# Softmax attention in one long stream: second-pass scores one position earlier, preparation spread over forty positions, first-pass scores multiplied twice

## The reference, cut to what matters

```python
sim = einsum('bhid,bhjd->bhij', q, k) / sqrt(hd)      # 4 sequences, 16 heads of width 8, n = 1024
sim = where(causal, neg, sim)
p = softmax(sim);  entropy = -sum(p * log(p + 1e-9))
beta = where(entropy > 0.5, maximum(poly(entropy), 1.0), 1.0)
attn = softmax(sim * beta)                            # a second softmax over the same scores
out = (attn @ v) @ Wo.T + bo
```

## Time and profile before

| what | us |
|---|---|
| median of 3 runs | 2694.11 (2691.54 to 2702.1) |
| the profiled execution | 2696.02 |
| its span | 2694.2 |
| first exp1 (L1175) to last one | 1006.5 to 2080.3 |

### The profile page before, as it was taken

How to read it: one execution, slowest core, us unless ns; L and a number is a source line. 1 busy time by engine, 2 the same in 40 slices (tenths; PEclk the granted TensorE clock), 3 DMA queues, 4 the chain that set the end, 5 groups by cost and what they waited for, 6 DMA issues and landing times. The chain is left out here.

```text
span 2694.2 us, 23532 instructions
## 1 busy us (share of the span) xinstructions
PE 1694.7 (63%) x6573; PEld 748.6 (28%) x6573; DVE 1548.0 (57%) x3577; ACT 1393.0 (52%) x2650; POOL 73.8 (3%) x71
## 2 busy tenths in 40 slices
PE   3544554899999944477777787677877642122172
PEld 2222332344444420122223222232222210111141
DVE  3444343445353449987788777977777134477411
ACT  2222222434343319888988999898989531000020
POOL 0000000000000010000000000000000000000314
PEclk9666666999999975566667656776667875555586
DMA  3000000555555510110101010201010100100212
GB/s 119 0 0 0 0 0 0 137 152 133 145 141 144 153 51 25 35 70 21 59 19 75 19 60 18 84 18 56 23 55 7 43 3 12 24 0 0 91 62 74
DMA packets 55812, 143.38 MB, mean 53 GB/s; under 512 B 7640, under 2 KB 22648, under 8 KB 53088
## 3 DMA queue, kind: packets, MB, share of 16 engines
q1 hardware_dynamic: 53648, 137.84, 17.3%
q0 software_dynamic: 2048, 4.20, 0.5%
HBM read 124.56 MB, written 17.45 MB: 53 GB/s over the span
## 5 line engine op out<-in xcount | busy, mean ns | idle before, releaser
L1273 DVE CUSTOM_DVE_ANT_0 sa_lg<-sa_e,sa_lg 128x1024 f32<-128x1024 f32 (+7 forms) x512 | 387.0, 756 | 162.6 <-ACT sa_lg L1185 162.6
L1053 PE MATMUL sa_ps<-sa_k1s,sa_q1s 72*128 72x512 bf16 (+3 forms) x768 | 297.2, 456 | 233.6 <-DVE sa_nmax L1264 197.0
L1175 ACT ACTIVATE sa_e<-sa_e,sa_nmax 128x1024 f32<-128x1024 f32 (+7 forms) x512 | 401.3, 784 | 48.6 <-DVE sa_nmax L1264 48.3
L1264 DVE CUSTOM_DVE_ANT_0 sa_e<-sa_ps,sa_mask 128x1024 f32<-128x1024 f32 (+7 forms) x512 | 385.3, 753 | 36.6 <-PE sa_ps L1053 34.9
L1185 ACT ACTIVATE sa_lg<-sa_e,sa_sum 128x1024 f32<-128x1024 f32 (+7 forms) x512 | 400.6, 782 | 2.7 <-DVE sa_prod L1273 2.2
L1193 ACT ACTIVATE sa_p<-sa_ps 128x512 f32<-128x512 f32 x576 | 336.5, 601 | 110.1 <-PE sa_ps L1087 55.8
L1084 PE MATMUL sa_ps<-sa_q2s,sa_k2s 75*128 75x512 bf16 (+3 forms) x768 | 299.9, 428 | 91.7 <-ACT sa_p L1193 70.1
L701 DVE TENSOR_TENSOR mx_hw<-mx_spread,mx_h 128x512 f32<-128x512 f32 x256 | 176.3, 691 | 252.2 <-ACT mx_h L608 242.5
L608 ACT ACTIVATE mx_h<-mx_ps 128x512 f32<-128x512 f32 (+1 forms) x264 | 156.7, 596 | 286.0 <-PE mx_ps L544 277.7
L544 PE MATMUL mx_ps<-mx_f,m 128*128 128x512 f32 x512 | 263.0, 595 | 1.7 <-ACT mx_h L608 1.7
L557 PE MATMUL mx_ps<-mx_hw,m 128*128 128x512 f32 x512 | 262.0, 594 | 1.7 <-DVE mx_hw L701 1.7
(11 more groups left out here) (287 smaller groups left out, 1952.4 us busy)
## 6 DMA issues: line engine op xcount, KB each, us to landing
mx_spread<-mx_spill SPq DMA_DIRECT2D x256, 256.0 KB, 4.0
sa_q1s<-sa_spill_q SPq DMA_DIRECT2D x96, 96.0 KB
sa_k1s<-sa_spill_k SPq DMA_DIRECT2D x96, 96.0 KB
sa_q2s<-sa_spill_q SPq DMA_DIRECT2D x48, 192.0 KB
sa_k2s<-sa_spill_k SPq DMA_DIRECT2D x48, 192.0 KB
m<-m_in SPq DMA_DIRECT2D x1, 4256.0 KB, 16.0
be_w<-w_in SPq DMA_DIRECT2D x16, 256.0 KB, 6.1
sa_spill_q<-sa_qp SPq DMA_DIRECT2D x4, 768.0 KB, 13.3
```

The source lines that it names most:

```text
L1053: last = nc.tensor.matmul(out[:, col:col + w], q_ring[:, c % 2, local, i * P:(i + 1) * P], k_ring[:, c % 2, local, col:col + w], start=Tru ...
L1175: nc.scalar.activation(e[:, u % 5, 0:w], e[:, u % 5, 0:w], ACT.Exp, scale=-1.0, bias=nmax[:, b % 2, i, h:h + 1], accum_out=sums[:, b % 2, ...
L1264: nc.vector.tensor_tensor_reduce(out=e[:, u % 5, 0:w], in0=slot_of("unit", u)[:, 0:w], in1=mask_wide[:, SEQ - w:SEQ], scale=1.0, scalar=3. ...
L1273: nc.vector.tensor_tensor_reduce(out=lg[:, u % 2, 0:w], in0=e[:, u % 5, 0:w], in1=lg[:, u % 2, 0:w], scale=1.0, scalar=0.0, op0=ALU.mult, ...
```

## The change

Four edits in the same block:

1. `score` runs its products twice into the same slot, with the same operands; the second run overwrites the first with the same numbers.
2. On PE the pieces of the second pass for position u + 1 are issued right behind the score at position u, ahead of `widen`, the shift, the preparation and the transposes of position u. Before they stood last, for position u.
3. The preparation of the next sequence moves from positions 75 to 90 of the current one to 13 to 52, with the splits dealt out two positions apart; its spills move from SP's positions 92 and 97 to 43 and 53. v stays at 106.
4. `split_q2` gets a scratch buffer of its own (`left2`).

```diff
+        left2 = sb("sa_left2", [P, SEQ])
...
-        A_AT, Q_AT, K_AT, V_AT = 83, 86, 88, 106
+        A_AT, Q_AT, K_AT, V_AT = 23, 33, 44, 106
...
-                    if (b := batch_at(u, 92)) is not None:
+                    if (b := batch_at(u, 43)) is not None:
                         spill_first("q", b, q_split, q_parts, spill_q, q_spilled)
-                    if (b := batch_at(u, 97)) is not None:
+                    if (b := batch_at(u, 53)) is not None:
                         spill_first("k", b, k_split, k_parts, spill_k, k_spilled)
...
-                    for col in range(0, keys, BANK):
+                    for col in (*range(0, keys, BANK), *range(0, keys, BANK)):
...
                     if u + AHEAD < ALL1:
                         score(u + AHEAD)
+                    for m in pieces2_at(u + 1):
+                        second(m)
+                        if m % GROUP == GROUP - 1 and m >= GROUP:
+                            answer(m // GROUP - 1)
+                    if group_at(u, 2) == ALL_GROUPS - 1:
+                        answer(ALL2 - 1)
                     if (k := side_at(u, WIDE_AT)) is not None:
                         widen(k)
...
-                    for m in pieces2_at(u):
-                        second(m)
-                        if m % GROUP == GROUP - 1 and m >= GROUP:
-                            answer(m // GROUP - 1)
-                    if group_at(u, 2) == ALL_GROUPS - 1:
-                        answer(ALL2 - 1)
...
-                    if (b := batch_at(u, 77)) is not None:
+                    if (b := batch_at(u, 16)) is not None:
                         ln.square(nc, act, b, 1)
-                    if (b := batch_at(u, 79)) is not None:
+                    if (b := batch_at(u, 18)) is not None:
                         ln.root(nc, act, b, 1, load=False)
...
-                    split_up(q_cm[k // 2 % 2][rows, :], left[rows, :], parts_of(q2_parts, rows), q2_split, steps)
+                    split_up(q_cm[k // 2 % 2][rows, :], left2[rows, :], parts_of(q2_parts, rows), q2_split, steps)
...
-                    if (b := batch_at(u, 75)) is not None:
+                    if (b := batch_at(u, 13)) is not None:
                         ln.total(nc, seq(b))
-                    if (b := batch_at(u, 76)) is not None:
+                    if (b := batch_at(u, 14)) is not None:
                         ln.subtract(nc, dve, b, 1, seq(b))
-                    if (b := batch_at(u, 78)) is not None:
+                    if (b := batch_at(u, 17)) is not None:
                         ln.variance(nc, dve, b, 1)
-                    if (b := batch_at(u, 80)) is not None:
+                    if (b := batch_at(u, 20)) is not None:
                         ln.scale(nc, dve, b, 1, y_tm[:, :, :])
...
                         take_q(b)
-                        split_q(b, range(0, 3))
-                    if (b := batch_at(u, Q_AT + 1)) is not None:
-                        split_q(b, range(3, 5))
+                    for r in range(5):
+                        if (b := batch_at(u, Q_AT + 1 + 2 * r)) is not None:
+                            split_q(b, range(r, r + 1))
...
-                    if (b := batch_at(u, K_AT + 1)) is not None:
-                        split_k(range(2, 4))
-                    if (b := batch_at(u, K_AT + 2)) is not None:
-                        split_k(range(4, 5))
+                    for r in range(2, 5):
+                        if batch_at(u, K_AT + 2 * r) is not None:
+                            split_k(range(r, r + 1))
```

## The result

The changed kernel is **slower**: 2744.94 us (median of 6 runs, 2733.69 to 2747.17) against 2697.95 us for the kernel before in the same comparison (6 runs); ratio 1.017, 95% interval 1.0149 to 1.0192. That is 47 us more, outside the range of the forecast. The profiled execution took 2744.51 us (span 2742.7); the one of before took 2696.02.

A forecast was written before the change was run, and what follows sets the result against it. ACT bounds the steady positions (1.96 us each), a 48.1 us chain from entropy to second pass the sides. Terms 19.6 - 6.6 - 13.5 - 6 + 2 + 2 = -2.5 us gave 2692 us, 8-in-10 range 2668 to 2732.

The forecast's parts named there:

- +19.6 for the first 64 positions: First sequence: preparation moved where DVE has little room, 14.6 us of work plus 2.5 and 2.5 of waits; bounds 14 and 25.
- -6.6 for the next 32: Positions 64 to 96: without the preparation they last 64.7 us behind the side's entropy instead of 71.4; bounds -3 and -9.
- the chain: From a side's entropy through splits, spill and loads to the next second pass's first piece: 48.1 us, said to bound the side.
- that is absorbed: DVE's standstill of 2.5 to 5.3 us at transposes behind pieces costs nothing, except before a side.
- four fifths of the time at the high level: Weighting of PE's clock at six sides, -2.2 us each high and +2.9 low; taken as -1 each, -6 us.
- 2.8 us of ACT's lead: At the seven other normalisings ACT has this lead and lacks up to 2.2 us at the low clock: +2 (0 to 15).
- the low branch: A side at PE's low clock: widening +1.6, logarithms -1.2, later entropy +2.5, together +2.9 us.
- Rival (b): Transposes and widening behind pieces that wait for ACT make DVE stand still: +38 in full, two thirds taken, 2720 us; chance 0.24.
- the low level should last short: With doubled scores PE has no pause at clock 0.5, so the high clock comes soon; +2 us (0 to 10).
- Rival (c): Doubled scores do not raise the clock, PE bounds steady positions at 34.0 against 31.3 us: +67, 2760 us or more; chance 0.07.
- No loss in the steady part: Doubled scores bring neither gain nor loss of their own in steady positions; only +2 us for single waits (0 to 10).
- the 2.5 us for doubled scores: First sequence: DVE waiting for doubled scores, 0.55 us in every 8 positions, partly covered, taken as 2.5 over 86 positions.

The follow-up runs named there:

- e3: Kernel before with only the preparation moved to positions 13 to 52 and the separate scratch buffer for split_q2: 2696.67 us, 0.9994.
- e5: Kernel before with PE issuing the second-pass pieces of position u + 1, but still last in position u: 2696.08 us, 0.9997.
- e6: Kernel before with PE issuing the pieces of position u itself first, right behind the score: 2699.28 us, 1.0003.
- e12: e11 with the pieces of position u + 1 issued last in position u: 2653.56 us, 0.9857 against the kernel before.
- e11: Kernel before with second-pass key and shift loads issued early and only the two later preparations moved to positions 13 to 52: 2679.32 us, 0.9935.
- e2: Kernel before with only the new PE order, pieces of position u + 1 right behind the score: 2723.3 us, 1.0088.
- e9: As e2 against the kernel before, but the transposes of the answers stay ahead of the pieces: 2702.11 us, 1.0023.
- e1: Kernel before with only the first-pass score products run twice: 2719.18 us, 1.008.

## Why the forecast was wrong, point by point

**Right: edit 3.** +19.6 for the first 64 positions (measured +21.3 with the doubled scores, +18.1 without), -6.6 for the next 32 (-6.0 and -6.7). For the later preparations the forecast kept 3 us of cost each and reckoned -13.5; e3 shows -20.3 in their old places and +10.1 in the halves where the work now lies, -10.2. The sum for edit 3 was -0.5; e3's ratio is -0.06%, some -2 us, with an interval from -6 to +3 us.

**Right in the main: the chain.** A visible wait of 4.96 us at a side, cut to about half, brought nothing in the whole time (e5, e6), and in the changed kernel the chain behind it still takes 46.8 to 48.2 us. That PE and ACT do not shorten it at all was too strong: e5's chain is 0.4 to 2.3 us shorter and its four sides are 5.9 us faster together. e12 against e11 shows the bound from the other side. The place to which ACT's wait went is the forecast one in e5, the group's first piece; in the changed kernel the trace shows the copy of the shift, two positions behind the widening (3.93 us, 31.2 in all eight sides), which the forecast did not name. The first piece is late as well (up to 3.0 us), but the copy stands in front of it.

**Wrong, first step: edit 2, "that is absorbed" and "four fifths of the time at the high level".** The forecast worked out, at position 254, that the transposes behind the pieces make DVE stand still for 2.5 to 5.3 us. Its own terms (1521.8, then 0.4, 1.06 and 1.3 to 1.9, against 1522.11) give 2.5 to 3.1; its 1525.0 and 1527.9 do not follow from them. In e2 the first twelve waits of the stream are 2.4 to 3.0 us, in the changed kernel only 1.0 to 2.5 (33.3 us in 14 places with two longer ones at the end, 3.9 and 6.1, of which the kernel before had one, 3.4). So the size was right for e2 and too high for the changed kernel.

The steps that failed are the next ones. "With 0.44 us to spare a position that is absorbed, except before a side" and 2.8 us of ACT's lead gave +2 for all other places; in e2 the stretches without a side are 10.5 us longer (7.5 in the five halves, 3.0 in the halves at 160 and 288), positions 64 to 96 another 3.0. For the six sides the forecast had -2.2 each at the high clock level, +2.9 at the low one, and weighed them four to one, for which no row spoke; that made -6. In the changed kernel all eight widenings took 3.49 to 3.68 us, at a granted clock of 0.50 to 0.55, and the one at the side at 128 began 10.1 us behind the entropy instead of 8.2; in e2 they took 3.20 to 3.68. There the entropy came 1.4 to 2.2 us later, as the low branch had it, and the six sides together cost 7.8 us. The tail, for which the forecast had no term, is 6.5 us longer, since its widening begins at +6.6 instead of +3.9 us behind the entropy. The forecast took -6 + 2 = -4; measured is +23 us (0.88%). Rival (b) is this mechanism, with a price for edit 2 of 33 us in full, of which it took two thirds: near what e2 shows. It had a chance of 0.24, and it stays 25 us short of the 2744.94 because it had nothing for edit 1 behind the first sequence.

The rule that was broken can be put in one line: PE executes its matmuls in the order in which they stand. The Trainium skill says so in "TensorE: Matmul & The Clock Gate", "Step-by-step: what each phase is for": only the weight loads are pulled ahead, the matmuls stay in program order. The trace agrees: e2 and e9 differ by nothing but the place of eight transposes in each group, and by 0.65%.

**Wrong, second step: edit 1, "the low level should last short".** The forecast's working for PE at the unchanged clock was 34.0 to 37.5 us for 31.3; from this it concluded that PE would have no pause at the low level, and from one pair of stretches in the earlier trace rows that a PE without a pause is granted the high clock soon. The second half does not hold. In the changed kernel:

```profile
1282.77:1303.25 20.48, 19.73 (x78) 7.07 (x79) 18.35 (x42) 19.54 (x40) 0.00 (x0) 0.50 0.18 50
```

20.48 us at 0.50, with PE busy for 19.73 of them, 14.18 of these without a pause in its records. The 3.41 us of the earlier trace rows was one case, not a rule. The doubled scores raised the clock in the stream to 0.72, in the steady positions from 0.58 to 0.73, and that does not pay for them: +19 us by the medians of e1, where the forecast had +2 with an upper bound of 10. Rival (c), PE the bound throughout, was +67; the truth lies between, as the clock rose in part. "No loss in the steady part" came true in the changed kernel (31.40 against 31.30 us, its pieces stand first), but not with the doubling alone (32.23 in e1). Most of e1's cost lies in the halves, 5 of them +7.6, in the two sides with the preparation, +6.1, and in positions 64 to 96, +2.8.

The Trainium skill, in "TensorE: Matmul & The Clock Gate", "Why this matters for your kernels", advises to keep TensorE free of long idle gaps. The trace agrees in the direction (0.66 to 0.74), but here the higher clock did not pay for what raised it: matmuls that are done only for the clock cost 0.8% on this kernel and 1.3% on the faster e12.

**The signs that the forecast had set.** Positions 0 to 64 at 110 us: 111.90, as stated, with ACT at 85%, but DVE at 92% (102.57) and not near 100%. Positions 64 to 96 at 70 (70.90), the 4.96 us gone and the chain at 46 to 49 (46.8 to 48.2): as stated. Normalising waits of 2.5 us or more, 14 times: 14 waits, but only two of them above 2.5. The granted clock in the steady part, 0.75 or more: 0.69 to 0.78 in the six stretches of sixteen positions, 0.73 in the one shown, just short. None of the three signs under which the sum was to be wrong showed (the chain below 45 us at the sides, the first 64 positions up by under 10, ACT below 95% in the steady part), and the sum was wrong: they did not watch the two terms that failed.

So the two misses have the same sign: +27 us from the place on PE and +17 us from the columns, by the medians: 44 of the 49.5 us between the forecast's -2.5 and the measured +47. Some 2 us of the rest are that the two together are slightly dearer than apart (1.7% against 1.6%); what is left is within the noise of the medians. What the misses share is an assumption: both terms counted on the high clock level, where the traces show the low one for the widenings and for much of the rest. Whether edit 2 would be free at the high level no run shows. The close agreement on edit 3 is in part luck: by itself, without the 2.5 us for doubled scores, its terms make -3; the ratio says -2, the cut of the one profiled execution +3, and its two larger parts missed by 3 and 1 us in the same direction.
